# Decoder layer: a new order and tiling of the cross attention's row maxima, with the gate's scores taken from eight added columns

## What is computed

```
x = layernorm(x + self_attention(x))               # 16 heads of 16
x = layernorm(x + differential_cross_attention(x, ctx))
      # per head two softmaxes over 8 + 8 channels: a1 - lam * a2, times v, then the output projection
x = layernorm(x + mixture_of_experts(x))           # scores = x @ gate_w.T, 8 experts, top 2
```

## Time and profile before

| | |
|---|---|
| time, median of 3 runs | 1747.01 us (1746.3 to 1747.81) |
| span of the profiled execution | 1765.9 us |
| PE / DVE / ACT / POOL busy, of that span | 89% / 63% / 51% / 43% |
| `front` (first instruction to the last query store) | 0 to about 438 us |
| `cross` up to the last score tile, then its tail | 438 to 1160, 1160 to 1200 us |
| `experts` and `finish` | 1200 to 1766 us |

### The profile page before, as it was taken

The page is one execution under the profiler, slowest core; times in us unless marked ns, Lnnn a source line. Parts: engine busy times, 40 slices in busy tenths (PEclk is TensorE's granted clock), DMA queues, the critical chain, the costliest instruction groups (busy, mean ns, idle before and its releaser), DMA issues. The chain is left out here.

```text
span 1765.9 us, 46393 instructions
## 1 busy us (share of the span) xinstructions
PE 1566.4 (89%) x17664; PEld 1193.8 (68%) x17664; DVE 1117.6 (63%) x2617; ACT 897.4 (51%) x2175; POOL 759.0 (43%) x916
## 2 busy tenths in 40 slices
PE   4899999995899998999899989847999999999991
PEld 2577777774466666666566666526888888888891
DVE  5566666664788888878877877643454444444443
ACT  2345544543466666666666656523444444444444
POOL 6334334432675555776577567530111211212212
PEclk9899999998799999999999989868999999999996
DMA  6666666653665555565455445237777777767744
GB/s 179 181 182 185 190 190 187 185 154 77 161 170 150 143 141 138 148 160 144 136 157 158 136 116 162 72 125 274 250 247 245 256 241 246 268 228 252 273 139 176
DMA packets 205509, 318.93 MB, mean 181 GB/s; under 512 B 61000, under 2 KB 174056, under 8 KB 205288
## 3 DMA queue, kind: packets, MB, share of 16 engines
q1 hardware_dynamic: 180648, 248.48, 46.8%
q0 software_dynamic: 21504, 66.19, 12.5%
q10 hardware_dynamic: 3136, 1.30, 0.3%
HBM read 224.52 MB, written 91.03 MB: 179 GB/s over the span
## 5 line engine op out<-in xcount | busy, mean ns | idle before, releaser
L1208 DVE TENSOR_REDUCE cross_mx<-cross_bank_max 112x2 f32<-112x750 f32 x512 | 457.9, 932 | 123.7 <-PE cross_bank_max L1323 120.4
L1021 ACT ACTIVATE cross_probs<-cross_bank_score 125x448 f32<-125x448 f32 x768 | 399.0, 546 | 255.0 <-PE cross_bank_score L1313 220.1
L1323 PE MATMUL cross_bank_max<-ckst,cqst 96*112 96x375 f16 x1024 | 265.2, 342 | 31.1 <-DVE cross_mx L1208 20.4
L1500 POOL DMA_INDIRECT acc<-experts_y,experts_dest_i x64 | 98.7, 1543 | 442.7 <-ACT experts_y L1537 372.4
L1577 DVE TENSOR_TENSOR experts_hid<-experts_bank_h,experts_gated 128x256 f32<-128x256 f32 (+1 forms) x288 | 113.6, 394 | 261.6 <-ACT experts_gated L1526 257.7
L1313 PE MATMUL cross_bank_score<-cqst,ckst 97*125 97x448 f16 x768 | 267.8, 368 | 9.2 <-ACT cross_probs L1021 6.4
L1609 PE MATMUL experts_bank_h<-experts_x_hi,experts_w_more 128*128 128x256 f16 (+1 forms) x1536 | 234.0, 264 | 0.0
L1323 PEld LDWEIGHTS cross_bank_max<-ckst,cqst 96*112 96x112 f16 x1024 | 116.6, 133 | 125.0 <-DVE cross_mx L1208 99.3
L1609 PE MATMUL experts_bank_h<-experts_x_lo,experts_w_more 128*128 128x256 f16 (+1 forms) x768 | 196.2, 264 | 0.0
L1526 ACT ACTIVATE experts_gated<-experts_bank_h 128x256 f32<-128x256 f32 (+1 forms) x288 | 103.7, 360 | 166.9 <-PE experts_bank_h L1609 163.4
L1339 PE MATMUL cross_bank_out<-cross_probs,cross_val 125*32 125x112 f32 x6144 | 181.2, 266 | 1.5 <-issue 1.5
(11 more groups left out here) (241 smaller groups left out, 3045.9 us busy)
## 6 DMA issues: line engine op xcount, KB each, us to landing
experts_w_more<-w_halves SPq DMA_DIRECT2D x24, 3072.0 KB, 12.2
w<-w_halves SPq DMA_DIRECT2D x12, 3072.0 KB, 12.6
cross_ew<-in_experts POOLq DMA_DIRECT2D x32, 768.0 KB
w_halves<-cross_ew_half POOLq DMA_DIRECT2D x32, 768.0 KB, 7.5
ckst<-cross_k SPq DMA_DIRECT2D x96, 187.5 KB
cross_v<-front_v SPq DMA_DIRECT2D x24, 531.2 KB
cross_val<-cross_v SPq DMA_DIRECT2D x32, 398.4 KB
front_src<-in_ctx_t SPq DMA_DIRECT2D x24, 500.0 KB, 8.9
```

Of the source, the lines that this page charges most:

```text
L1021: nc.scalar.activation(probs[:, e % PROBS], bank_score[e % 2][0:SC, 0:4 * T], ACT.Exp, scale=CROSS_SCALE).then_inc(probs_ready, 1)
L1208: nc.vector.tensor_reduce(mx[:, b % nb, 2 * n:2 * n + 2], bank_max[n % 2][0:T, :, 0:S], AX.X, ALU.max).then_inc(max_read, 1)
L1323: last = nc.tensor.matmul(bank_max[n % 2][0:T, i, 0:S], qst[0:STACK, p, u // 4, (u % 4) * T:(u % 4 + 1) * T], kst[0:STACK, p, u // 4, :], ...
```

## The change

Four things are done.

1. **Maxima in stripes of 128.** A batch's 32 x 112 = 3584 query columns are cut into 28 stripes of 128 instead of 32 units of 112; two stripes make a pair, 14 pairs per batch (`PAIRED`). Four stripes lie across the border of two groups, and are two matmuls of 64 query columns each, into PSUM partitions 0 to 63 and 64 to 127. DVE reduces 128 partitions; the row transfers carry 16 x 128 values, of which the last two lanes are overwritten by the next one, and `slot_of` reverses the ring of query stacks for that.
2. **Gate scores without turned rows.** The norm's mean drops out if the gate's weights are centred, so scores = rstd x (r @ centred gate). `front` makes centred gate weights once, folds them through the output projection (`w_gate`), and its `query` step computes x1 @ centred gate (six matmuls of 8 columns per batch), which DVE adds up into `x_gate` and SP stores beside x1. In `cross` the projection has 264 columns instead of 256, and POOL multiplies the 8 added ones with rstd. The steps `turn` and `score` with their two reads on ACT go.
3. **Scaling on ACT.** The scaling of the experts' weights by 64 moves from POOL to ACT (`scale_weights`, at parts 7, 11, 17); `ew` and `ew_half` get two buffers.
4. **New places** in the parts for every step, read, evacuation and pair.

```diff
-STEP_AT = {"turn": (1, -2), "row1": (4, 0), "score": (6, -2), "out1": (8, -1), "heads": (13, -1),
-           "row0": (15, 1), "proj": (17, -1), "out0": (21, 0)}
-EVACUATE_AT = ((14, 0), (2, -1))
-AGGREGATE_AT, NORMALISE_AT = 19, 23
+STEP_AT = {"row1": (2, 0), "out1": (5, -1), "heads": (10, -1), "row0": (13, 1), "proj": (16, -1), "out0": (22, 0)}
+READ_AT = {"row1": (2, 0), "out1": (6, -1), "heads": (12, -1), "row0": (14, 1), "proj": (15, -1), "out0": (21, 0)}
+EVACUATE_AT = ((13, 0), (1, -1))
+AGGREGATE_AT, NORMALISE_AT = (20, -1), (23, -1)
+SCALE_AT = (7, 11, 17)
+MAX_AT = (0, 2, 3, 4, 6, 9, 11, 12, 14, 14, 17, 18, 21, 23)
+REDUCE_AT = (0, 2, 3, 4, 6, 9, 11, 12, 14, 14, 17, 18, 21, 23)
+def stripe(j):
+    lo, hi, wide = LANES * j, LANES * (j + 1), 4 * T
+    cuts = sorted({lo, hi, *(g * wide for g in range(GROUPS) if lo < g * wide < hi)})
+    return [(a // wide, a % wide, a - lo, b - a) for a, b in zip(cuts, cuts[1:])]
...
                     for i in range(2):
-                        u = 2 * n + i
-                        last = nc.tensor.matmul(bank_max[n % 2][0:T, i, 0:S], qst[0:STACK, p, u // 4, (u % 4) * T:(u % 4 + 1) * T],
-                                                kst[0:STACK, p, u // 4, :], start=True, stop=True)
+                        for g, col, lane, size in stripe(2 * n + i):
+                            last = nc.tensor.matmul(bank_max[n % 2][lane:lane + size, i, 0:S], qst[0:STACK, slot_of(b), g, col:col + size],
+                                                    kst[0:STACK, p, g, :], start=True, stop=True)
...
                         for k in range(KD):
-                            last = nc.tensor.matmul(bank[0:T, 0:D], heads_t[:, p, k], w_out[:, k, :], start=k == 0, stop=k == KD - 1)
-                    elif name == "turn":
-                        wait(pe, y_ready, b + 1)
-                        for k in range(KD):
-                            last = nc.tensor.transpose(bank[:, k * T:(k + 1) * T], rows[:, b, 128 * k:128 * k + 128], ident[0:T, 0:T])
-                    elif name == "score":
...
+                            last = nc.tensor.matmul(bank[0:T, 0:D + EXP], heads_t[:, p, k], w_out[:, k, :], start=k == 0, stop=k == KD - 1)
...
+                        pool.tensor_tensor(score[:, b], r[:, p, D:], small[:, p, 1:2].to_broadcast([T, EXP]), ALU.mult).then_inc(score_ready, 1)
...
-                        pool.tensor_scalar(ew_big[:, cols], ew[:, cols], WSCALE, None, ALU.mult).then_inc(ew_big_ready, 1)
                         wait(pool, ew_big_ready, n)
...
+                def scale_weights(b, i):
+                    cols = slice(i * piece, (i + 1) * piece)
+                    wait(act, ew_loaded[b % 2], 16 * (b // 2 + 1))
+                    wait(act, ew_ready, pieces * (b - 1) + i + 1)
+                    nc.scalar.activation(ew_big[:, cols], ew[:, b % 2, cols], ACT.Copy, scale=WSCALE).then_inc(ew_big_ready, 1)
```

In `front`, the query step and the one-time work (SP issues three loads at turn -3; PE averages at turn -2 and folds at turn 0):

```diff
+                        terms = [(k, gt, yt) for k in range(KD) for gt, yt in ((gate_hi, y_hi), (gate_lo, y_hi), (gate_hi, y_lo))]
+                        for at, (k, gt, yt) in enumerate(terms):
+                            last = nc.tensor.matmul(bank[0:T, KD * T:KD * T + EXP], yt[:, p, k], gt[:, k],
+                                                    start=at == 0, stop=at == len(terms) - 1)
...
+                            nc.vector.scalar_tensor_tensor(out=x_gate[:, b % nb], in0=bank_of("query")[0:T, KD * T:KD * T + EXP], scalar=1.0 / WSCALE,
+                                                           in1=gate_b, op0=ALU.mult, op1=ALU.add)
...
+                        sp.dma_start(x1[bass.ts(b, T), D:], x_gate[:, b % nb]).then_inc(gate_stored[b % nb] if on(b + 1) else last_query, 16)
...
+                def average_gate():
+                    pe.wait_ge(gate_loaded, 16 * 3)
...
+                def fold_gate():
+                    pe.wait_ge(gate_ready, 2)
```

More of the change, by code:

```diff
@@ L171, in front @@
         q_lo = ph.sb("q_lo", [128, nb, KD, T], F16)
+        spare = lambda i, lo, n: w[:, i].rearrange("p k n -> p (k n)")[:, lo:lo + n]
+        by_k = lambda t, n: t.rearrange("p (k n) -> p k n", k=KD)
+        gate, gate_c, gate_big = (by_k(spare(0, 16 * i, KD * EXP), EXP) for i in range(3))
+        gate_b = spare(0, 48, EXP)[0:T]
+        mean = spare(0, 128, 128)
+        back = w[:, 1]
+        back_b = spare(3, 0, KD)
+        back_bt = by_k(spare(2, 0, KD * T), T)
+        gate_hi = ph.sb("gate_hi", [128, KD, EXP], F16)
+        gate_lo = ph.sb("gate_lo", [128, KD, EXP], F16)
+        x_gate = ph.sb("x_gate", [T, nb, EXP], F32)
+        gate_stored = ph.sems("gate_stored", nb)
         bank_max = ph.ps("bank_max", [128, 512])
@@ L866, in load @@
                     if b == B - 1:
-                        wait(sp, last_query, 32)
+                        wait(sp, last_query, 48)
                     if b >= 2:
@@ L889, in _ @@
                     if c == B:
-                        wait(sp, ew_stored, 16 * CUTS)
+                        for p in range(2):
+                            wait(sp, ew_stored[p], 16 * CUTS // 2)
                         sp.dma_start(w.rearrange("p q h n -> p q (h n)"),
@@ L905, in _ @@
             def _(pool):
-                pool.dma_start(ew[:], a["experts"][0]).then_inc(ew_loaded, 16)
+                pool.memset(b_out[:, D:], 0.0).then_inc(w_gate_ready, 1)
+                for b in range(2):
+                    pool.dma_start(ew[:, b], a["experts"][b]).then_inc(ew_loaded[b], 16)
                 pool.memset(val[:, :, CHUNKS * VROW:], 0.0).then_inc(stacks_ready, 1)
@@ L1034, in _ @@
                             nc.scalar.activation(lam[:, 2:4], lam[:, 0:2], ACT.Exp).then_inc(lam_ready, 1)
-                        for name in ("turn", "row1", "score", "heads", "row0"):
+                        for name in ("row1", "heads", "row0"):
                             at, lag = READ_AT[name]
@@ L1111, in route @@
                     if at == 2:
-                        wait(dve, read["score"], hi)
+                        wait(dve, score_ready, hi)
                         dve.wait_ge(route_consts, 12)
@@ L1373, in step @@
                             wait(pe, consts_loaded, 16 * consts)
+                            pe.wait_ge(w_gate_ready, 2)
                         wait(pe, read["heads"], b + 1)
                         for k in range(KD):
-                            last = nc.tensor.matmul(bank[0:T, 0:D], heads_t[:, p, k], w_out[:, k, :], start=k == 0, stop=k == KD - 1)
-                    elif name == "turn":
-                        wait(pe, y_ready, b + 1)
-                        for k in range(KD):
-                            last = nc.tensor.transpose(bank[:, k * T:(k + 1) * T], rows[:, b, 128 * k:128 * k + 128], ident[0:T, 0:T])
-                    elif name == "score":
-                        wait(pe, read["turn"], b + 1)
-                        for k in range(KD):
-                            last = nc.tensor.matmul(bank[0:T, 0:EXP], y_t[:, p, k], gate_w[:, k, :], start=k == 0, stop=k == KD - 1)
+                            last = nc.tensor.matmul(bank[0:T, 0:D + EXP], heads_t[:, p, k], w_out[:, k, :], start=k == 0, stop=k == KD - 1)
                     last.then_inc(full[name], 1)
@@ L1409, in _ @@
                             scores(c, e)
-                        n = maximum_at(e)
-                        if n is not None and on(c + lead):
+                        for n in at_part(MAX_AT, e) if on(c + lead) else ():
                             maxima(c + lead, n)
```

201 lines of the change are left out of this document (134 added, 67 removed).

## The result

| | before | after |
|---|---|---|
| time, median | 1746.65 us (4 runs, 1745.85 to 1747.81) | 1707.03 us (4 runs, 1700.65 to 1712.41) |
| ratio | | 0.9769, 95% interval 0.974 to 0.9798 |
| span of the profiled execution | 1765.9 us | 1706.5 us (its own time 1708.24) |

The kernel is 39.6 us faster; 1702 was forecast, 5 us from the median. The changed kernel, run again for the experiments, gave 1707.14 (ratio 0.9745).

The account below looks back on a forecast made before the run. Bound: the alternation in `cross`, where DVE and ACT starve in PE's bursts and are late between them. Turns -55, ends of `cross` -4.4, `front` +14 give -45 us, applied to the median: 1702 us, range 1675 to 1735.

Parts of the forecast that it names:

- The turn, 19.3: Steady part of `cross`: a turn falls from 21.06 to 19.3 us, -55 us over 31 turns.
- The walk: New order of a `cross` turn followed, burst to burst: 18.6 us together, put at 19.3 for being 4% short.
- Its split into work and waits: Steady turn of `cross`: of 1.8 us gained, 1.3 are PE's work and 0.5 waits.
- Split stripes, 0: PE in `cross`: two matmuls of 64 columns count as one, shape changes cost at most 0.4 us per turn, taken as 0.
- rival (a): `cross`: split halves run one after the other and shape changes cost, 1.0 us per turn, +32, 1734 us; chance 14%.
- Ends of `cross`, -4.4: Before the first score tile two reductions fewer, -1.8 us; in the tail scores come sooner, -2.6; together -4.4.
- A scaling waiting for POOL or a load: Sign in the profile after that would show the prediction wrong; no size given.
- `front`, +14: `front`: 0.3 us per batch over 32 batches, 10 us, plus 4 us of one-time work; +14 (7 to 23).
- the one-time part: Start of `front`: PE waits for three later loads, then small products with DVE's instructions; 4 us (2 to 7).
- The tail, -2.6: End of `cross`: POOL makes the last batch's scores beside the norm, about 0.2 us instead of 2.8: -2.6.
- (b): `cross`: ACT becomes the bound, its 6.0 us of waits stay, turn 22.3 us, +47, 1794 us; chance 8%.
- (c): `cross`: only the work is gained, waits stay at 3.25 and rise, turn 20.3, -14, 1733 us; chance 10%.

Follow-up runs that it names:

- old_places_pool: The changed kernel with pairs, steps, reads and evacuations at their old places and the experts' weights scaled on POOL again: 1734.19 us (ratio 0.9926), turn 20.50.
- joined: The changed kernel with every stripe one matmul of 128 query columns, also the four across a border of two groups: 1702.49 us (ratio 0.973), turn 19.01.
- the fresh pair: Second profiles of the unchanged kernels before and after, compared stage by stage: spans 1752.2 and 1708.6 us.
- scale_on_pool: The changed kernel with the experts' weights scaled on POOL again instead of ACT: 1694.59 us (ratio 0.9666), quiet turn 19.10.

## Why the prediction was right, and where it was not

- **The turn, 19.3: right, 19.10.** PE's, DVE's and ACT's totals were close: DVE is busy 15.4 and ACT 15.4 in a turn (15.5 and 15.3 forecast). The walk gave the spans to within 0.3 us. It said 18.6 together, where its four spans add up to 18.7, and the 4% added for its shortness came out as 2.7%.
- **Its split into work and waits: wrong.** "Of the 1.8 us gained, 1.3 are PE's work and 0.5 waits." With 1.0 us for split stripes PE's stream fell by about 0.3. The turn fell by 1.96, so the larger part is waits, and old_places_pool says which step removed them: the new work in the old places gave 0.56, the new places 1.40. The sum held because the walk priced the order, not because the split was understood.
- **Split stripes, 0: wrong in price, right in effect.** I read from the burst that pieces run side by side, which they do, and that a change of shape costs at most 0.05; it costs 0.21 to 0.28 per stripe, 1.0 per turn. That is rival (a)'s 1.0 us, though not from halves one after the other. Rival (a) erred in putting it on the path: joined gave back 0.1 us per turn, not 1. That so much of it would fall into waits the prediction had not worked out, so the small effect was luck.
- **Ends of `cross`, -4.4: the step that failed.** The start came out at +7.4 instead of -1.8. I costed the scalings on ACT in the steady turn alone, where they are free, and did not follow ACT's stream through the turns before the first batch, where five of them stand ahead of the first negated row and wait for POOL and a load. "A scaling waiting for POOL or a load" was among the prediction's own signs of being wrong, and it came. From front's last turned rows to the first score tile 32.2 us pass instead of 23.3.
- **`front`, +14: right, +11.3 in the fresh pair**; per batch 0.24 undisturbed (0.3 forecast); the one-time part +1.3 to +5.4 in the profiles (4, range 2 to 7).
- **The tail, -2.6: -1.8 measured** with the experts and the end.
- Two errors cancelled: the turns gave 6 us more than forecast, the start of `cross` 9 less.
- **Rivals.** (b): ACT's wait for scores fell from 6.0 to 2.9 per turn. It is 5.9 in old_places_pool (97.4 us in 340) and 3.6 in scale_on_pool (71.5 in 380), so the new places took 2.3 of it and the scalings filled 0.7. (c): waits did not stay. What holds the turn at 19.10 is not one engine: 1.0 us less on PE gives 0.1, 1.3 less on ACT nothing, both together 0.1, two more reductions and pairs cost 0.48. Which alternation sets it stays open.

## What to carry to other kernels

Cost a moved step in the turns before the steady state as well: an in-order engine that has nothing to do there will still stand in front of the one thing that the pipeline's start waits for. An order table is priced by walking the stream through a whole turn, for totals of busy time say little about it; and a transfer's place must leave time for it to land behind whatever bulk transfer an engine off the path may start at that moment. Before explaining a gain, undo the parts one at a time: here the parts that looked large (split stripes, ACT's load) moved the turn by 0.1 us or nothing.

## What the runs showed of the hardware

- Matmuls in separate columns of the array start side by side, two of 64 or four of 32 alike. Going in and back costs 0.21 to 0.28 us of PE's time, of which 0.09 is the way in.
- A DVE instruction on 8 columns took 995 ns instead of 167 when both operands were in SBUF and POOL was busy there; all 21 of them ended 20 to 25 ns behind POOL's instruction.
- A 4 KB transfer landed after 1.6 us on quiet queues and after 6 us behind a 768 KB store and a batch's loads. PE stood idle 2.2 us for it, then the granted clock was 0.50 (1.2 GHz) and a burst took 2.47 us instead of 1.36.
